# A fused two-layer kernel on one core: GpSimd's order of work, an inverse root by a power on GpSimd, and a conversion spread over two units

## What is computed

```python
ln_out = _ln(hidden_states, ln_w, ln_b)
q = _ln(_fp8_linear_pertensor(ln_out, wq, ...).reshape(b, s, g, hpg, d), qln_w, qln_b)
k = _ln(_fp8_linear_pertensor(ln_out, wk, ...).reshape(b, s, g, d), kln_w, kln_b)
v = _fp8_linear_pertensor(ln_out, wv, ...)
core = _gqa(q, k, v)            # softmax(q k^T / sqrt(d)) v, 16 heads, 8 groups, d = 128
xout = _gqa(_ln(qx), _ln(kx), vx)   # the same with keys and values from the context
catq = _div_clamp_fp8(concatenate([core, xout]), proj_smooth)
return einsum(catq, wproj) * (proj_in_scale * proj_w_scale)
```

## Time and profile before

| what | value |
|---|---|
| median of 3 runs | 1187.11 us (1186.66 to 1187.77) |
| the profiled execution, its own time | 1185.83 us |
| its span, first to last instruction | 1184.0 us |
| DVE busy, share of the span | 957.7 us, 81% |
| PE busy | 894.8 us, 76% |
| ACT busy | 723.2 us, 61% |
| POOL busy | 401.2 us, 34% |
| DVE busy on the sums of squares (L1254 x128) | 121.8 us, 951 ns each |
| POOL busy on `cat` (L1231 x128) | 147.6 us, 1153 ns each |

### The profile page before, as it was taken

How to read it: one execution, slowest core, us unless ns; L and a number is a source line. 1 busy time by engine, 2 the same in 40 slices (tenths; PEclk the granted TensorE clock), 3 DMA queues, 4 the chain that set the end, 5 groups by cost and what they waited for, 6 DMA issues and landing times. The chain is left out here.

```text
span 1184.0 us, 22559 instructions
## 1 busy us (share of the span) xinstructions
PE 894.8 (76%) x6878; PEld 785.4 (66%) x6878; DVE 957.7 (81%) x2509; ACT 723.2 (61%) x2536; POOL 401.2 (34%) x602
## 2 busy tenths in 40 slices
PE   3620576218878799878879988888899999997638
PEld 3620243217777688767778877777799999996627
DVE  7989898788888899788889877777788888886461
ACT  3442244647777777677777766666777777774313
POOL 0029000003343433344343444444444443433124
PEclk9855598559999999999999999999999999999559
DMA  6030000111001011000101100000000000000400
GB/s 216 1 107 0 0 1 0 36 47 34 2 1 37 2 37 37 2 1 1 37 1 37 46 10 10 10 10 10 10 15 11 15 10 15 11 6 1 147 19 19
DMA packets 24292, 29.97 MB, mean 25 GB/s; under 512 B 1584, under 2 KB 19824, under 8 KB 23920
## 3 DMA queue, kind: packets, MB, share of 16 engines
q1 hardware_dynamic: 23792, 27.51, 7.1%
q0 software_dynamic: 384, 1.05, 0.3%
HBM read 25.93 MB, written 2.62 MB: 24 GB/s over the span
## 5 line engine op out<-in xcount | busy, mean ns | idle before, releaser
L1477 PE MATMUL a_pj_ps<-wp,a_cat 128*128 128x256 f32 x1024 | 157.6, 297 | 91.8 <-POOL a_cat L1231 91.8
L1254 DVE TENSOR_REDUCE a_v<-a_sq 128x6 f32<-128x768 f32 x128 | 121.8, 951 | 116.1 <-ACT a_sq L1407 115.9
L1477 PEld LDWEIGHTS a_pj_ps<-wp,a_cat 128*128 128x128 f32 x1024 | 131.0, 192 | 112.5 <-POOL a_cat L1231 105.9
L1231 POOL TENSOR_TENSOR a_cat<-a_tb,a_mb 128x512 fp32r<-128x512 bf16 x128 | 147.6, 1153 | 63.5 <-DVE a_tb L1293 61.5
L1389 ACT ACTIVATE a_p<-a_kT_sc_ps,a_nmax 128x64 f32<-128x64 f32 x512 | 151.5, 307 | 2.9 <-DVE a_nmax L1261 2.9
L1443 PE MATMUL a_qo_ps<-wq,a_xqf 128*128 128x512 f32 x512 | 151.2, 417 | 0.0
L1218 POOL TENSOR_TENSOR a_pn<-a_p,a_rsum 128x256 f32<-128x256 f32 x128 | 78.8, 616 | 183.8 <-DVE a_rsum L1338 183.8
L1400 ACT ACTIVATE a_sq<-a_kv_ps 128x256 f32<-128x256 f32 x128 | 49.2, 384 | 135.2 <-PE a_kv_ps L1505 66.9
L1535 PE MATMUL a_kT_sc_ps<-a_kT,a_qT 128*128 128x64 f32 x1024 | 128.8, 269 | 0.6 <-ACT a_kT L1403 0.6
L1535 PEld LDWEIGHTS a_kT_sc_ps<-a_kT,a_qT 128*128 128x128 f32 x1024 | 124.3, 192 | 1.2 <-ACT a_qT L1395 1.0
L1389 ACT ACTIVATION_READ_ACCUMULATOR a_p<-a_kT_sc_ps,a_nmax 128x1 f32 x512 | 103.3, 202 | 0.0
(11 more groups left out here) (315 smaller groups left out, 2197.5 us busy)
## 6 DMA issues: line engine op xcount, KB each, us to landing
a_ctx<-in_ctxT SPq DMA_DIRECT2D x32, 128.0 KB, 2.2
w_work<-in_wprojT SPq DMA_DIRECT2D x3, 1024.0 KB, 5.7
x_res<-in_x SPq DMA_DIRECT2D x4, 512.0 KB, 5.4
vT<-in_ctxT SPq DMA_DIRECT2D x2, 1024.0 KB, 9.8
w_work<-in_wqxT SPq DMA_DIRECT2D x2, 1024.0 KB, 5.0
w_work<-in_wkvxT SPq DMA_DIRECT2D x4, 512.0 KB, 4.6
out_x<-x_res SPq DMA_DIRECT2D x4, 512.0 KB, 4.6
tf_work<-in_wqT SPq DMA_DIRECT2D x1, 1024.0 KB, 6.5
```

Source lines behind the costliest of these rows:

```text
L1231: nc.gpsimd.tensor_tensor(cat[out8.n % 2][:], tb[:], mb[:], ALU.subtract).then_inc(cat_ready, 1)
L1254: norm(nc.vector.tensor_reduce(v6[:], sq[:].rearrange("p (h d) -> p h d", d=D), AX.X, ALU.add))
L1477: last = nc.tensor.matmul(pj_ps[:, pj.turn % 2, :], cat[pj.n % 2][:, a * P:(a + 1) * P], wp[part][:, pj.half * HU + a, :], start=(pj.half ...
```

## The change

Five things are done together.

1. POOL's head of a step is that of unit s-1 instead of unit s (`head_item(norm)`).
2. The inverse deviation is one instruction on POOL, first in its step: `r6` = `v6` to the power of `minus_half`, a tile of -0.5. It waits for DVE's sums of the same unit (`sums_ready`) and for the keys of the unit before, which read `r6`. DVE's mean-and-epsilon step, its three Newton steps and ACT's logarithm and exponential are gone, and the sums wait for the power of the unit before.
3. `sq` has 129 columns for each head, the last of them set to 128 x 1e-5 once at the start of the stage, so that the sum over a row holds epsilon. ACT writes the squares into the first 128. The factor sqrt(128) that is now missing from `r6` is put into the queries' and keys' weights (`lnp`, `kln_w`) at the start.
4. `convert` takes thirds. In self phases the cast of 768 elements becomes three of 256: one in the unit of half 0, two in that of half 1. In cross phases the cast of 256 stays in half 0, and the context's cast and remainder go to half 1. PE counts three thirds to a turn.
5. With the Newton steps gone, clip, exponent bits and rounding constant follow each other on DVE with nothing between.

```diff
-    scale = float(D) ** -0.5
+    root = float(D) ** 0.5
+    scale = 1.0 / root
...
-        lnp = sb("lnp", [P, 2, 2])
+        lnp, kln_w = sb("lnp", [P, 2, 2]), sb("kln_w", [P, 2])
...
-        sq = sb("sq", [P, QW + KW])
-        v6, r6, t6, l6 = (sb(nm, [P, HU + GU]) for nm in ("v6", "r6", "t6", "l6"))
-        g6 = sb("g6", [P, HU + GU])
+        sq = sb("sq", [P, HU + GU, D + 1])
+        v6, r6, minus_half = (sb(nm, [P, HU + GU]) for nm in ("v6", "r6", "minus_half"))
...
-                pool.wait_ge(cleared, 1)
-
-                def convert(turn):
+                nc.gpsimd.memset(minus_half[:], -0.5).then_inc(cleared, 1)
+                pool.wait_ge(cleared, 2)
...
+                def convert(turn, third):
...
-                    q0, nq = (0, 3 * KC) if cross < 0 else (3 * KC, KC)
-                    nc.gpsimd.tensor_copy(xqf[par][:, 0:nq, :], xq8[:, q0:q0 + nq, tile * P:(tile + 1) * P]
-                                          ).then_inc(xqf_ready, 1)
-                    if cross >= 0:
+                    if cross < 0:
+                        for a in third:
+                            nc.gpsimd.tensor_copy(xqf[par][:, a * KC:(a + 1) * KC, :],
+                                                  xq8[:, a * KC:(a + 1) * KC, tile * P:(tile + 1) * P]
+                                                  ).then_inc(xqf_ready, 1)
+                        return
+                    if 0 in third:
+                        nc.gpsimd.tensor_copy(xqf[par][:, 0:KC, :], xq8[:, 3 * KC:4 * KC, tile * P:(tile + 1) * P]
+                                              ).then_inc(xqf_ready, 3)
+                    if 2 in third:
                         pool.wait_ge(ctx_in[par], 16 * (cross // 2 + 1))
                         nc.gpsimd.tensor_copy(ctx_p[par][0][:], ctx_t[par][:]).then_inc(ctx_upper, 1)
                         pool.wait_ge(ctx_upper, cross + 1)
                         nc.gpsimd.tensor_tensor(ctx_p[par][1][:], ctx_t[par][:], ctx_p[par][0][:].bitcast(F32),
                                                 ALU.subtract).then_inc(ctx_ready, 1)
 
-                convert(0)
+                convert(0, (0, 1, 2))
                 for s in range(UNITS + 4):
-                    u, soft, out8 = At(s), At(s - 3), At(s - 4)
+                    u, norm, soft, out8 = At(s), At(s - 1), At(s - 3), At(s - 4)
+                    if norm.live:
+                        pool.wait_ge(sums_ready, norm.count())
+                        wait_unit(pool, kn_ready, norm.before(1))
+                        nc.gpsimd.tensor_tensor(r6[:], v6[:], minus_half[:], ALU.pow).then_inc(r_ready, 1)
                     if soft.live:
                         pool.wait_ge(rsum_ready, soft.count())
                         pool.wait_ge(exp_ready, soft.count(4))
...
-                    head = head_item(u) if u.live else None
+                    head = head_item(norm) if norm.live else None
                     if head:
                         pool.wait_ge(aw["head_scaled"], head.count)
...
                         pool.wait_ge(cadd_ready, out8.count())
                         wait_unit(pool, pj_done, out8.before(2))
                         nc.gpsimd.tensor_tensor(cat[out8.n % 2][:], tb[:], mb[:], ALU.subtract).then_inc(cat_ready, 1)
-                    if u.live and u.half == 0 and u.turn + 1 < N_PHASES * NT:
-                        wait_unit(pool, kv_done, u.before(1))
-                        wait_unit(pool, q_done, u.before(1))
-                        convert(u.turn + 1)
+                    if u.live and u.turn + 1 < N_PHASES * NT:
+                        if u.half == 0:
+                            wait_unit(pool, kv_done, u.before(1))
+                            wait_unit(pool, q_done, u.before(1))
+                        convert(u.turn + 1, (0,) if u.half == 0 else (1, 2))
...
-                    prep.mark(nc.vector.tensor_scalar(lnp[:, i, :], col(f"q{pre}ln_w", 0, 2), scale, None, ALU.mult))
+                    prep.mark(nc.vector.tensor_scalar(lnp[:, i, 0:1], col(f"q{pre}ln_w"), scale * root, None, ALU.mult))
+                    prep.mark(nc.vector.tensor_scalar(lnp[:, i, 1:2], col(f"q{pre}ln_b"), scale, None, ALU.mult))
+                for i, pre in enumerate(("", "x")):
+                    prep.mark(nc.vector.tensor_scalar(kln_w[:, i:i + 1], col(f"k{pre}ln_w"), root, None, ALU.mult))
+                prep.mark(nc.vector.memset(sq[:, :, D:D + 1], D * LN_EPS))
...
-                    def norm_guess():
-                        norm.at(u.count(3, 0))
+                    def squares_sums():
                         dve.wait_ge(sqq_ready, u.count())
                         dve.wait_ge(sqk_ready, u.count())
-                        norm(nc.vector.tensor_reduce(v6[:], sq[:].rearrange("p (h d) -> p h d", d=D), AX.X, ALU.add))
-                        nc.vector.tensor_scalar(v6[:], v6[:], 1.0 / D, LN_EPS, ALU.mult, ALU.add
-                                                ).then_inc(var_ready, 1)
+                        wait_unit(dve, r_ready, u.before(1))
+                        nc.vector.tensor_reduce(v6[:], sq[:], AX.X, ALU.add).then_inc(sums_ready, 1)
...
-                    def newton(part):
-                        if part == 0:
-                            dve.wait_ge(rs_ready, u.count())
-                            dve.wait_ge(var_ready, u.count())
-                            norm.mark(nc.vector.scalar_tensor_tensor(t6[:], g6[:], -0.5, g6[:], ALU.mult, ALU.mult))
-                        elif part == 1:
-                            norm.settle()
-                            norm.mark(nc.vector.tensor_tensor(t6[:], t6[:], v6[:], ALU.mult))
-                        else:
-                            norm.settle()
-                            nc.vector.scalar_tensor_tensor(r6[:], t6[:], 1.5, g6[:], ALU.add, ALU.mult
-                                                           ).then_inc(r_ready, 1)
...
                     if u.live:
-                        norm_guess()
+                        squares_sums()
                     if sm.live:
                         maxima()
                     if pv.live:
                         scaled_output()
                         round8(0)
-                    if u.live:
-                        newton(0)
-                    if pv.live:
                         round8(1)
-                    if u.live:
-                        newton(1)
-                    if pv.live:
                         round8(2)
                     if sm.live:
                         dve.wait_ge(exp_ready, sm.count(4))
                         wait_unit(dve, pn_ready, sm.before(1))
                         nc.vector.reciprocal(rsum[:], psum_s[:]).then_inc(rsum_ready, 1)
                     if u.live:
-                        newton(2)
                         normalised_query()
...
-                    u, norm, sm, pv = (At(s - b) for b in (0, 1, 2, 3))
-                    if norm.live:
-                        chain.at(norm.n)
-                        act.wait_ge(var_ready, norm.count())
-                        chain(nc.scalar.activation(l6[:], v6[:], ACT.Ln))
-                        wait_unit(act, r_ready, norm.before(1))
-                        nc.scalar.activation(g6[:], l6[:], ACT.Exp, scale=-0.5).then_inc(rs_ready, 1)
+                    u, sm, pv = (At(s - b) for b in (0, 2, 3))
...
-                        wait_unit(act, var_ready, u.before(1))
-                        nc.scalar.activation(sq[:, QW:QW + KW], kv_bank(u)[:, 0:KW], ACT.Square).then_inc(sqk_ready, 1)
+                        wait_unit(act, sums_ready, u.before(1))
+                        nc.scalar.activation(sq[:, HU:HU + GU, 0:D], kv_bank(u)[:, 0:KW].rearrange("p (h d) -> p h d", d=D),
+                                             ACT.Square).then_inc(sqk_ready, 1)
...
-                        nc.scalar.activation(kT[:], kT_ps, ACT.Identity, scale=col(f"k{pre}ln_w"),
+                        nc.scalar.activation(kT[:], kT_ps, ACT.Identity, scale=kln_w[:, i:i + 1],
...
-                        nc.scalar.activation(sq[:, 0:QW], q_bank(u), ACT.Square).then_inc(sqq_ready, 1)
+                        nc.scalar.activation(sq[:, 0:HU, 0:D], q_bank(u).rearrange("p (h d) -> p h d", d=D), ACT.Square
+                                             ).then_inc(sqq_ready, 1)
...
                         if u.half == 0:
-                            pe.wait_ge(xqf_ready, u.turn + 1)
+                            pe.wait_ge(xqf_ready, 3 * (u.turn + 1))
```

More of the change, by code:

```diff
@@ L1130, in attention_stage @@
         prep = k["dve_chain"]
-        own_consts = prep.n + 4
+        own_consts = prep.n + 9
         ctx_in, ctx_upper, ctx_ready = [sg(f"ctx_in{i}") for i in range(2)], sg("ctx_upper"), sg("ctx_ready")
@@ L1136, in attention_stage @@
         sqq_ready, sqk_ready, v_ready = sg("sqq_ready"), sg("sqk_ready"), sg("v_ready")
-        var_ready, rs_ready = sg("var_ready"), sg("rs_ready")
+        sums_ready = sg("sums_ready")
```

(21 more changed lines are left out.)

## The result

The changed kernel takes 1086.38 us (median of 4 runs, 1084.92 to 1087.60) against 1187.44 us for the kernel before (4 runs). The ratio is 0.9146, with a 95% interval of 0.9129 to 0.9163: 101 us faster. The forecast was 1093 us with a range of 1088 to 1130.

The account below looks back on a forecast made before the run. A ring of ACT's head, POOL's head, `cat` and PE bound the kernel; afterwards PE alone. 1185.8 us with -96.9 + 2.0 + 0.4 + 0.2 = -94.3 gave 1091.5, plus 1.3 to the median: 1093 us, range 1088 to 1130.

Parts of the forecast that it names:

- the residual: On DVE in front of `tb` every fourth unit, 0.74 us: 2 us lost over some 12 self units with a piece.
- costed at nothing: The first three head units, in the start-up, were taken to gain nothing from the move of POOL's head.
- The head one unit later: On POOL: the wait for ACT's head goes and units with heads run at PE's own pace, 96.9 us gained.
- My margin of -0.16 us: Self units with piece and residual: `cat`'s time to spare before PE wants it, 0.43 + 0.15 - 0.74 us.
- three casts and constants: Start of the stage: 0.4 us lost as PE waits for three casts, 0.2 us for five small instructions more.
- The power's price: POOL's power on six columns takes 0.5 us, with ends of 0.19 and 3 us, and costs nothing.
- The room by its result: Self units with a piece: by its result alone, the power on POOL is free up to 1.6 us.
- The rival that decided from 0.68 us: The power holds DVE's clip, so a POOL-DVE ring of 4.72 us plus the power sets the pace; chance 0.18.
- The thirds and the epsilon column: POOL's conversion in thirds and DVE's six more elements in a 0.95 us reduction: each taken to cost nothing.

Follow-up runs that it names:

- e1: The kernel before with one edit, POOL's head of a step being that of unit s-1: 1089.54 us, ratio 0.9181.
- e2: The changed kernel with the head of unit s back on POOL: 1193.73 us, ratio 1.0067.
- e6: The kernel before with POOL's head one unit later and the conversion in thirds, Newton steps kept on DVE and no power: 1090.15 us.
- e10: The changed kernel without the four projection matmuls of the weights' lower halves in each unit: 1046.10 us.
- e11: The kernel before with POOL's head one unit later, without the four projection matmuls of the weights' lower halves: 1057.18 us.
- e4: The changed kernel with the power done twice in a row, the first into a spare tile: 1164.72 us.
- e7: The changed kernel with a second power, on one column only, in front of the power: 1096.16 us.
- e5: The changed kernel with a POOL product of 512 bf16 elements in SBUF in front of the power: 1149.05 us.
- e3: The changed kernel with the whole conversion in the unit of half 0 again: 1086.03 us.

## Why the prediction was right or wrong

The mechanism was right; three sizes and the low end of the range were wrong. The terms of the sum that failed are the residual (2.0 us lost; PE lost nothing there that can be seen) and the start-up "costed at nothing" (it gave 1.1 us). The low end then left no room for scatter between executions, which was worth 3.1 us. From 1093 to the measured 1086.4 it is 6.6 us: 1.5 in the stretches with heads and the eight units behind them (94.9 forecast with the residual's loss, 96.4 measured), 0.4 in the eight units from self to cross, 1.1 in start-up, 0.3 ahead of the first sums, 1.6 outside the stage, 1.5 between the profiled execution and the median, and rounding.

**The head one unit later: right.** 96.9 us were forecast for the stretches with heads and the eight units behind them. The same stretches give 142.08 - 114.06 = 28.0, 161.71 - 129.29 = 32.4, 176.44 - 140.90 = 35.5 and 0.4 us, in all 96.4. e1 shows how much of this is the head's move alone: 27.63 + 31.12 + 35.54 + 0.00 = 94.3 us; e2 shows that without it nothing is gained. The other 2.1 us come with the power (e6). The clock was 1.00 throughout these stretches, as expected.

**The residual in every fourth unit: wrong.** I had 2.0 us lost, with bounds of 0 and 4. Against 5.40 us each, the self units with heads lost 0.7 us in the first phase (114.06 - 113.40) and gained 0.3 in the second (129.29 - 129.60). Neither is the residual's: PE waits for `cat` only once in these stretches, 0.2 us, and the units with the residual and a piece find `cat` just in time (the rows under e6). My margin of -0.16 us had the residual at its duration of 0.74 us; from its start to the next instruction's it is 346.07 - 345.41 = 0.66. It also had 0.15 us gained by the missing Newton steps; from the sums to the end of `cat`, e1 takes 348.96 - 342.00 = 6.96 and the changed kernel 348.39 - 341.63 = 6.76 us, 0.20 gained. The loss that I had forecast is there in e1, where it is 0.15 us of waiting. The 5.40 us of one unit was itself a little high: PE's own pace in the second self phase is 5.38 to 5.39.

**Start-up costed at nothing: wrong.** "The first three head units lie in the start-up and are costed at nothing" missed that there PE is not yet full, and that the way from the squares to the queries counts. Units 0 to 4 take 16.23 against 17.34 us, and e1 and e6, with Newton steps, keep the 17.3: 1.1 us that the power brings. That PE does not set the time there is shown by e10 and e11: with less work for PE the same units take 16.25 and 17.34 us. I also had 0.6 us for three casts and constants; from POOL's first memset of the stage to the first sums it was 0.3 more than before, since casts in a row follow each other by 0.34 us and not by 0.42.

**Scatter between executions: not in the range.** Of the 4.9 us by which the profiled execution (1086.55 us) beat my 1091.5, 0.9 us lie ahead of the stage (the memset of its start at 259.58 in place of 260.51 us) and 0.7 behind its last sums, nearly all of it in code that is the same; over all the profiles the stage's first sums start anywhere from 262.8 to 266.6 us. And the 1.3 us that I added from the profiled execution to the median was not there this time: the median is 0.2 us below it. My low end of 1088 allowed for the residual's 2 us and start-up and tail, but for no scatter, although three runs of the kernel before lay 1.1 us apart. Said afterwards, 2 us for that would just have held.

**The power's price: wrong by 2.7 times, without effect.** I took 0.5 us, from thirty elementary passes at 1.6 ns; one column costs a hundred times that (0.16 us), and the fixed part is 0.565 - 0.16 = 0.41 us and not 0.19. That it came out harmless was luck, two errors against each other. The room by its result is real (1.6 us forecast, 1.74 by e4 and e7). The rival that decided from 0.68 us, the power that holds DVE's clip, is ruled out: at 1.35 us it would have cost, by its own formula, (4.72 + 1.35 - 5.40) = 0.67 us in each of 44 units and in all some 45 us. In the changed kernel the clip takes 293 ns at the median and 296 at most in 128 units, and in 125 of them the power runs beside it. Before, the 57 clips that ran beside nothing on POOL took 293 to 296 ns, and the 69 beside `cat` about 0.61 us on the mean. The changed kernel's line (minimum, median, maximum):

```profile
L1282 DVE TENSOR_SCALAR a_yb<-a_yb x128: 293/293/296, 279.2 to 992.5; 128x512 bf16<-128x512 bf16 x128
```

and that of the kernel before:

```profile
L1281 DVE TENSOR_SCALAR a_yb<-a_yb x128: 293/548/659, 280.3 to 1090.6; 128x512 bf16<-128x512 bf16 x128
```

So the row of `cat` and the clip was read rightly (e5 repeats it with another instruction), but it did not carry over to the power. That the power touches SBUF for only a small part of its 1.35 us is my reading and not shown; of the 122 DVE instructions of the same kind (clip, exponent bits, rounding constant) that run across a power's end in the changed kernel, two, begun 0.18 to 0.19 us ahead of it, take 0.33 and 0.34 us (one of them at 333.41 in the unit above), and the other 120 stay under 0.30. The rule of the Trainium skill's page "SBUF — State Buffer", section "Who interferes with whom", that the pair is held for a whole instruction, agrees with `cat` and with e5; for the power the trace disagrees, though it reads SBUF too and begins first (332.27, the clip 333.08).

**The thirds and the epsilon column: right** as costed at nothing (e3; the sums take 958 ns in place of 951).

## What to carry to other kernels

When an in-order engine's step waits for something fresh in front of work that is long ready, look for the ring that this closes; moving it by one stage of the pipeline was worth 94 of the 98 us here, and all the rest 3 to 4. Cost a slow instruction on a helper engine by the ring through its result, read from one unit's timeline, and put it behind work that is waited for anyway. A row that shows one instruction holding another prices only instructions of the same kind: `cat` and a product of 512 elements held DVE's clip, a power on six did not. Where instructions follow each other without a gap, count them by the spacing of their starts and not by their durations (0.66 against 0.74 us for the residual). The range has to hold the scatter between runs even where every term has been bounded.

## What the runs showed of the hardware

- A power on GpSimd takes 0.565 us on one column and 0.16 us for each further column of 128 partitions (1.35 us for six), where a product on one column takes 0.19 us.
- It does not hold VectorE's clip (two-byte, in SBUF): 293 to 296 ns in the 125 units where both run together. Of the 122 such instructions that run across the power's end two took 0.33 to 0.34 us. A GpSimd product of 512 elements holds the clip to 0.15 us past its end (888 ns on the mean in e5).
- GpSimd casts in a row: 0.40 us alone, 0.74 us for a pair, 0.34 us for each that follows.
